# Rows of x loaded behind their written blocks, statistics in slots 6, 0 and 1, the last nine head groups turned on TensorE, reciprocals stored with one DMA

## What is computed

```python
ln = layernorm(x)                                # statistics over 512 columns
q, k, v = split(ln @ w_qkv + b)                  # second layer: k, v of ctx
scores = q @ k.T / sqrt(32)
scores = scores * mask - 10000.0 * (1.0 - mask)
probs = softmax(scores)                          # exponentials times one reciprocal per row
x = x + merge_heads(probs @ v) @ w_o + b_o
```

## Time and profile before

| | |
|---|---|
| median of 3 runs | 2039.5 us (2033.07 to 2039.91) |
| the profiled execution | 2038.9 us, of it 2036.6 us span |
| mean granted TensorE clock | 0.993 |
| first stage, attention, perceptron | to about 105, to about 1300, to 2036.6 us |

### The profile page before, as it was taken

How to read it: one execution, slowest core, us unless ns; L and a number is a source line. 1 busy time by engine, 2 the same in 40 slices (tenths; PEclk the granted TensorE clock), 3 DMA queues, 4 the chain that set the end, 5 groups by cost and what they waited for, 6 DMA issues and landing times. The chain is left out here.

```text
span 2036.6 us, 41925 instructions
## 1 busy us (share of the span) xinstructions
PE 1981.6 (97%) x13584; PEld 1571.3 (77%) x13584; DVE 1471.5 (72%) x3874; ACT 1156.5 (57%) x3239; POOL 554.8 (27%) x562
## 2 busy tenths in 40 slices
PE   9999999999999999999999997999999999999998
PEld 8877777777776777777777775788888888888887
DVE  7799999999998899899898987465344443435333
ACT  4388788888888888887887876422212121112111
POOL 1022222222233343333324342053031231314000
PEclk9999999999999999999999998999999999999999
DMA  8546566667667767667676756432212212121201
GB/s 276 164 96 135 146 169 138 136 157 168 134 170 187 185 165 178 163 157 179 156 164 168 177 134 162 153 101 65 80 33 77 49 60 73 42 75 46 64 24 47
DMA packets 670394, 257.41 MB, mean 126 GB/s; under 512 B 483072, under 2 KB 614784, under 8 KB 670208
## 3 DMA queue, kind: packets, MB, share of 16 engines
q1 hardware_dynamic: 551936, 240.42, 44.4%
q10 hardware_dynamic: 118272, 14.69, 4.8%
HBM read 170.56 MB, written 84.41 MB: 125 GB/s over the span
## 5 line engine op out<-in xcount | busy, mean ns | idle before, releaser
L1316 ACT ACTIVATE A_p<-A_p,A_nmax 128x256 f32<-128x256 f32 x1024 | 506.9, 500 | 4.0 <-DVE A_res L1594 1.7
L1628 DVE CUSTOM_DVE_ANT_0 A_p<-A_p,A_ma 128x256 f32<-128x256 f32 x1024 | 375.1, 421 | 4.7
L1618 DVE TENSOR_TENSOR A_p<-A_sc,A_mk 128x1024 f32<-128x1024 f32 x256 | 312.1, 1219 | 77.1 <-PE A_tp L1078 58.2
L829 POOL TENSOR_TENSOR A_ct_l<-A_cx,A_ct_h 128x256 fp32r<-128x256 f32 x128 | 119.8, 936 | 724.4 <-DVE A_nmax L1628 694.3
L1333 ACT ACTIVATE A_pt<-A_tp 128x512 f32<-128x512 f32 x384 | 212.9, 588 | 59.5 <-PE A_tp L1078 58.3
L1078 PEld LDWEIGHTS A_tp<-A_ident,A_p 128*128 128x128 f32 x1536 | 176.8, 143 | 71.5 <-ACT A_p L1316 35.5
L1078 PE MATMUL A_tp<-A_ident,A_p 128*128 128x128 f32 x1536 | 221.0, 281 | 1.1 <-DVE A_xt_l L1577 0.7
L1316 ACT ACTIVATION_READ_ACCUMULATOR A_p<-A_p,A_nmax 128x1 f32 x1024 | 196.9, 192 | 0.0
L1465 ACT ACTIVATE A_mk<-A_tp,A_cols 128x512 f32<-128x512 f32 x62 | 42.7, 689 | 269.0 <-PE A_tp L70 269.0
L1465 ACT ACTIVATE A_ma<-A_tp,A_cols 128x512 f32<-128x512 f32 x62 | 42.8, 690 | 242.4 <-PE A_tp L70 242.4
L68 PE MATMUL A_banks<-A_xt_h,A_w_h 128*128 128x512 f32 x384 | 162.8, 424 | 5.9 <-DVE A_res L1594 5.3
(11 more groups left out here) (247 smaller groups left out, 5009.1 us busy)
## 6 DMA issues: line engine op xcount, KB each, us to landing
exponentials<-A_p SPq DMA_DIRECT2D x512, 64.0 KB, 2.3
A_pt<-exponentials SPq DMA_DIRECT2D x128, 256.0 KB, 4.2
A_x<-x SPq DMA_DIRECT2D x96, 256.0 KB, 3.8
A_res<-x SPq DMA_DIRECT2D x64, 256.0 KB, 3.0
A_rt<-inverses SPq DMA_DIRECT2D x512, 32.0 KB, 2.0
x<-A_res SPq DMA_DIRECT2D x64, 256.0 KB, 4.5
turned<-A_x ACTq DMA_DIRECT2D x224, 64.0 KB, 2.8
inverses<-A_turned_inv SPq DMA_DIRECT2D x512, 1.0 KB
```

Of the source, the lines that this page charges most:

```text
L829: pool.tensor_tensor(ct_l[:, f, part], cx[:, :], f32(ct_h[:, f, part]), ALU.subtract).then_inc(c_lo, 1)
L1316: act.activation(p[:, g % 2, j, t, :], p[:, g % 2, j, t, :], ACT.Exp, scale=-1.0, bias=nmax[:, g % 2, j, t:t + 1], accum_out=rsum[:, g % 2 ...
L1618: dve.tensor_tensor(p[:, g % 2, heads, :, :].rearrange("p j t s -> p j (t s)"), sc[:, heads, :], m, ALU.mult)\
L1628: dve.tensor_tensor_reduce(out=a_, in0=a_, in1=ma[:, b, t, :], scale=-1.0, scalar=BIG, op0=ALU.add, op1=ALU.min, accum_out=nmax[:, g % 2, ...
```

## The change

Four edits in one.

1. SP loads rows of the block after next as soon as their tile has been written out: tiles 0 and 1 in slot 5, tiles 2 and 3 in slot 6, ahead of `load_pair` in both, behind the semaphore `st_a` that `load_pair` waits for as well. DVE takes the statistics of tiles 0 and 1 at the end of slot 6, of tile 2 in slot 0 and of tile 3 in slot 1.
2. The reciprocals are stored by one DMA of all 128 partitions x 32. In DRAM they now lie as they came out of the block transposition, so the loads into `rt` take four pieces of 64 elements per partition where they took two of 128, and `scaled` reads `rt` in another order.
3. For the last nine groups (`KEPT`, 119 to 127; they are turned in slots (15,4) to (16,4)) all four heads are turned on PE and copied by ACT. Their block transposition, four stores and one load by DMA are gone.
4. In block 16 the low half `ct_l` is made by DVE, no longer by POOL.

```diff
+    KEPT = range(GROUPS - 9, GROUPS)
...
+        def moved(grp):
+
+            return int(grp not in KEPT)
+
+        def moves(grp):
+
+            return sum(moved(n) for n in range(grp))
+
+        def turns(grp):
+
+            return grp * HPG - moves(grp)
...
             def load_rows(k, r, some=range(TT)):
                 for t in some:
-                    wait(sp, x_lo, (r - 1) * TT + (t + 1))
+                    if by_blocks(k - 2):
+                        sp.wait_ge(st_a[t // 2], (turned_before(k - 2, r - 2) + 1) * TPB * (P // 32) * DMA)
+                    else:
+                        wait(sp, x_lo, (r - 1) * TT + (t + 1))
...
-                for n in range(P // 32):
-                    sp.dma_start(inv_dram[g % 2][:, n * 32:(n + 1) * 32], turned_inv[n * 32:n * 32 + TPB * HPG, g % 2, :])\
-                        .then_inc(st_i, DMA)
+                sp.dma_start(inv_dram[g % 2], turned_inv[:, g % 2, :]).then_inc(st_i, DMA)
...
-                wait_apart(sp, st_i, (grp + 1) * (P // 32) * DMA, cx_ok, grp)
+                wait_apart(sp, st_i, (grp + 1) * DMA, cx_ok, grp)
+                blocks = inv_dram[g % 2].rearrange("(n c) s -> n (c s)", c=32).rearrange("(a n) s -> a n s", a=1)
                 for j in range(HPG):
                     rr = slice(j * HD, (j + 1) * HD)
-                    own = inv_dram[g % 2].rearrange("(t j) s -> j t s", j=HPG)[j:j + 1]
-                    sp.dma_start(rt[rr, :].rearrange("p (t s) -> p t s", t=TPB), own.broadcast_to([HD, TPB, P]))\
-                        .then_inc(ld_i, DMA)
+                    own = blocks[:, :, j * TPB * 32:(j + 1) * TPB * 32]
+                    sp.dma_start(rt[rr, :].rearrange("p (n s) -> p n s", n=P // 32),
+                                 own.broadcast_to([HD, P // 32, TPB * 32])).then_inc(ld_i, DMA)
...
+                if own and moved(group(r, h, -1)[0]):
+                    load_exponentials(r, h, pv)
                 if own:
-                    load_exponentials(r, h, pv)
                     store_inverses(r, h)
                     if h == 6 and 0 < k < NU:
                         for t in range(2):
                             load_res(k - 1, r - 1, t + 2)
-                if exists(k, h, 0):
+                if exists(k, h, 0) and moved(group(r, h, 0)[0]):
                     store_exponentials(r, h)
                 if own:
...
-                if h == 0 and 0 < k < NU:
-                    load_rows(k + 1, r + 1, (2, 3))
-                if h == 7 and k + 1 < NU:
+                if k == 1 and h == 0 or by_blocks(k) and h == 6:
+                    load_rows(k + 1 + h // 6, r + 1 + h // 6, (2, 3))
+                if k == 0 and h == 7 or by_blocks(k) and h == 5:
                     load_rows(k + 2, r + 2, (0, 1))
...
-                if exists(k, h, -2):
+                if exists(k, h, -2) and k < NU:
                     weighed(r, k, h)
...
-                pe.wait_ge(pt_ok, (grp + 1) * TURNS)
-                pe.wait_ge(ld_p, (grp + 1) * DMA)
+                pe.wait_ge(pt_ok, turns(grp + 1))
+                wait(pe, ld_p, moves(grp + 1) * DMA)
...
-                    for i in range(2, TURNS):
+                    for i in range(2, HPG - moved(group(r, h, -1)[0])):
                         turn(r, k, h, i)
...
-                first = TPB * MOVED
-                if now:
-                    for n in range(first):
-                        exponential(r, k, h, n)
-                if own:
-                    for i in range(TURNS if bare else 2):
-                        turned_out(r, h, i)
+                leads = now and moved(group(r, h, 0)[0])
+                held = HPG - moved(group(r, h, -1)[0]) if own else 0
+                if leads:
+                    exponential(r, k, h, 0)
+                    exponential(r, k, h, 1)
+                for i in range(held if bare else min(held, 2)):
+                    turned_out(r, h, i)
+                if now and not leads:
+                    exponential(r, k, h, 0)
+                    exponential(r, k, h, 1)
                 if leaves and not late(k, h):
                     weighed(r, k, h)
-                if now:
-                    exponential(r, k, h, first)
-                if own and not bare:
-                    for i in range(2, TURNS):
+                if leads:
+                    exponential(r, k, h, 2)
+                if not bare:
+                    for i in range(2, held):
                         turned_out(r, h, i)
+                if now and not leads:
+                    exponential(r, k, h, 2)
                 unit_out(a_, k)
                 if now:
-                    for n in range(first + 1, 5):
-                        exponential(r, k, h, n)
+                    exponential(r, k, h, 3)
+                    exponential(r, k, h, 4)
...
-                if heads.start < MOVED:
-                    wait(dve, st_p, (grp - 1) * (P // 32) * DMA)
-                if heads.stop > MOVED:
-                    wait(dve, turned, (grp - 2) * TURNS + heads.stop - MOVED)
+                if grp > 1:
+                    if part == 0:
+                        wait(dve, st_p, moves(grp - 1) * (P // 32) * DMA)
+                    dve.wait_ge(turned, turns(grp - 2) + heads.stop - moved(grp - 2))
...
-                dve.tensor_tensor(cx[:, :], banks[:, pv[0], 0:S], rt[:, :], ALU.mult).then_inc(cx_ok, 1)
+                in_order = lambda ap: ap.rearrange("p (t n s) -> p t n s", t=TPB, n=P // 32)
+                dve.tensor_tensor(in_order(cx[:, :]), in_order(banks[:, pv[0], 0:S]),
+                                  rt[:, :].rearrange("p (n t s) -> p t n s", t=TPB, n=P // 32), ALU.mult).then_inc(cx_ok, 1)
+
+            def weighed(r, k, h):
+                grp, _, g = group(r, h, -2)
+                b, f = g // KT, g % KT
+                part = slice(b * S, (b + 1) * S)
+                dve.wait_ge(c_hi, grp + 1)
+                dve.tensor_tensor(ct_l[:, f, part], cx[:, :], f32(ct_h[:, f, part]), ALU.subtract).then_inc(c_lo, 1)
...
-                if exists(k, h, 0):
+                if exists(k, h, 0) and moved(group(r, h, 0)[0]):
                     exponentials_in_blocks(r, h)
                 if coming:
                     maxima(r, k, h, 0)
+                if leaves and k == NU:
+                    weighed(r, k, h)
...
-                if k < NU and h in ((0, 1) if k else (1, 2)):
-                    row_statistics(r + 1, 0 if h == (0 if k else 1) else 2)
-                    row_statistics(r + 1, 1 if h == (0 if k else 1) else 3)
+                if k < 2 and h in (1 - k, 2 - k):
+                    row_statistics(r + 1, 0 if h == 1 - k else 2)
+                    row_statistics(r + 1, 1 if h == 1 - k else 3)
+                if by_blocks(k) and h == 6:
+                    row_statistics(r + 2, 0)
+                    row_statistics(r + 2, 1)
+                if 1 < k < NU and h in (0, 1):
+                    row_statistics(r + 1, 2 + h)
```

## The result

The ratio is 1.0067, with a 95% interval of 1.0043 to 1.0091, or +13.7 us on 2039.5. The forecast was 2020 us, faster than before; it came out 0.7% slower.

What follows compares the result with a forecast made beforehand. The prediction took TensorE, busy 97% of the span, to bound the kernel. Its terms, -12 (`A_pt` waits), -4 (`A_k_l` waits), +8.4 (earlier rows) and -10.9 (end of attention), summed to -18.5 us, giving 2020 us, range 2004 to 2042.

## What to carry to other kernels

When a transfer is moved earlier, list every transfer that lands behind it and who waits for each of those landings, and take the slack of each from the trace. The price is set by the one with the least slack, not by the free share of the DMA engines; here it was most of all the load of `A_pt`, which had 1.6 to 1.8 us and lost 1.9 to 3.4. Put transfers that nobody waits for soon at the end of a slot's list; here that one change of order was worth 28 us. A bound taken from a landing in another slot holds only if something waits for it equally soon there.

## What the hardware showed

- Two 256 KB row loads ahead in SP's queue, at a DMA share of 0.85 to 0.92 in block 12, made the 256 KB stores of slot 5 land in 5.9 us at the median and the 512 KB load of turned rows in 5.6. With the row loads behind them these were 5.1 and 4.6 us, and 4.7 and 4.2 in the kernel before.
- A second queue by itself gave no protection. With the row loads on ScalarE's queue SP waited 49.3 us for the stores' landings, with them ahead in its own queue 49.3 too, with them behind in its own queue 20.0. Stores of exponentials issued together with the row loads landed in 4.1 instead of 2.8 us.
- Twice as many pieces of half the size (256 bytes) made the 32 KB loads of `rt` land in 2.2 instead of 2.0 us.
